# Delta stage: the gram products moved between the product through the state and the decay sums, and the block columns spread over six of eight chains

## The reference, cut to what matters

```python
# every token goes to 2 of 4 experts; each expert has a state S of 64x64 per head, 8 heads
def step(S, x):
    qt, kt, vt, bt, gt = x
    S = S * jnp.exp(gt)[..., None, None]
    kv = jnp.einsum('bhk,ebhkv->ebhv', kt, S)
    delta = (vt[None] - kv) * bt[..., None]
    S = S + kt[None, :, :, :, None] * delta[..., None, :]
    ot = jnp.einsum('bhk,ebhkv->ebhv', qt * scale, S)
    return (S, ot)
```

## Time and profile before

| | |
|---|---|
| runs | 3308.52, 3281.15, 3309.49 us; median 3308.52 |
| profiled execution | 3279.67 us, its span 3277.6 us, mean granted clock 0.964 |
| PE busy | 3008.8 us, 92% of the span |
| DVE busy | 1696.9 us, 52% |
| ACT, POOL busy | 1052.2 and 1480.7 us |
| the chain that ended last | 78% PE, 11% DVE, 4% issue, 3% ACT, 2% DMA |
| DVE L2114 and L2111 (block columns) | 114.5 and 98.7 us busy, 240 instructions each |
| the delta stage | from 1341 to 2012 us of the span |

### The profile page before, as it was taken

One profiled execution on the slowest core, in us unless ns is written; L12 is line 12 of the kernel. 1 busy time (PEld: TensorE's weight loads), 2 busy tenths in 40 slices (PEclk: granted clock), 3 DMA queues, 4 the chain that ended last, 5 costly groups with the idle time before them and its releaser, 6 DMA issues.

```text
span 3277.6 us, 45758 instructions
## 1 busy us (share of the span) xinstructions
PE 3008.8 (92%) x16145; PEld 1701.1 (52%) x16145; DVE 1696.9 (52%) x3820; ACT 1052.2 (32%) x2245; POOL 1480.7 (45%) x1466
## 2 busy tenths in 40 slices
PE   7999999888899899879999998998999999999828
PEld 3434566577677544457777765444533333444414
DVE  7633266488244432377766642442257777621361
ACT  2312422297122222233444432221034444432201
POOL 0565656498554447422222202554656666300003
PEclk9999999999999999999999989999999999999958
DMA  5400001110111244433444445311167666600404
GB/s 170 138 19 6 7 25 53 46 65 14 41 46 49 69 140 165 155 106 107 116 114 117 118 136 161 96 52 48 31 202 202 205 198 197 158 16 26 171 9 129
DMA packets 275957, 321.34 MB, mean 98 GB/s; under 512 B 155807, under 2 KB 193569, under 8 KB 275732
## 3 DMA queue, kind: packets, MB, share of 16 engines
q1 hardware_dynamic: 219684, 182.57, 18.5%
q0 software_dynamic: 51840, 134.60, 13.6%
q10 hardware_dynamic: 4208, 1.25, 0.2%
HBM read 215.75 MB, written 104.60 MB: 98 GB/s over the span
## 4 chain that ended last, share of the span: by engine, by line
PE 78%; DVE 11%; issue 4%; ACT 3%; DMA 2%; POOL 0%; SPq 0%; ACTq 0%; DVEq 0%; POOLq 0%
PE bank L2665 8%; PE bank L1520 5%; PE bank L2657 5%; PE bank L706 4%; PE bank L1299 3%; PE bank L2328 3%; PE bank L2819 3%; PE bank L2812 3%; PE bank L437 3%; PE bank L1115 3%; DVE delta_tmp L2111 2%; PE bank L729 2%; DVE delta_Us L2114 2%; PE bank L760 2%; PE bank L2308 2%
## 5 line engine op out<-in xcount | busy, mean ns | idle before, releaser
L2637 POOL DMA_INDIRECT conv_src<-xn_rows,keep x288 | 272.2, 945 | 175.3 <-DVE conv_msg L2703 109.4
L289 POOL DMA_INDIRECT sorted_bias<-perf_rec,place x256 | 259.2, 1012 | 146.5 <-PE bank L706 92.1
L2665 PE MATMUL bank<-conv_msg,conv_hot 128*128 128x512 f32 x576 | 272.0, 595 | 0.6 <-ACT conv_msg L2684 0.6
L1902 POOL TENSOR_TENSOR delta_dec<-delta_dec,rates_of 128x512 f32<-128x512 f32 x64 | 67.4, 1053 | 359.9 <-ACT delta_dec L1944 359.9
L2703 DVE TENSOR_TENSOR conv_msg<-bank,conv_src 128x512 f32<-128x512 f32 x288 | 185.5, 686 | 46.7 <-PE bank L2657 46.7
L664 POOL DMA_INDIRECT sorted_edge<-rec,place x128 | 126.7, 990 | 141.9 <-PE bank L1360 75.2
L2684 ACT ACTIVATE conv_msg<-conv_msg 128x1024 f32<-128x1024 f32 x144 | 152.0, 1055 | 102.0 <-DVE conv_msg L2703 102.0
L1115 PE MATMUL bank<-bias_prod,bias_hot 128*128 128x256 f32 x640 | 148.5, 388 | 25.2 <-issue 10.5
L2657 PE MATMUL bank<-conv_we,conv_eT 64*128 64x512 f32 x576 | 164.5, 648 | 0.7 <-ACT conv_eT L2681 0.7
L1099 POOL TENSOR_TENSOR bias_prod<-bias_col,bias_rec 128x512 f32<-128x512 f32 x128 | 146.9, 1177 | 17.1 <-PE bank L1115 16.4
L1115 PEld LDWEIGHTS bank<-bias_prod,bias_hot 128*128 128x128 f32 x640 | 120.4, 193 | 53.7 <-issue 28.6
(11 more groups left out here) (494 smaller groups left out, 6557.0 us busy)
## 6 DMA issues: line engine op xcount, KB each, us to landing
keep<-slot_qkv SPq DMA_DIRECT2D x32, 512.0 KB, 3.8
delta_kv<-slot_qkv SPq DMA_DIRECT2D x32, 512.0 KB, 3.8
sorted_edge<-sort_pad SPq DMA_DIRECT2D x8, 1440.0 KB
keep<-sorted_edge SPq DMA_DIRECT2D x18, 640.0 KB, 4.9
slot_out<-delta_o SPq DMA_DIRECT2D x64, 128.0 KB, 1.7
conv_src<-xn_rows,keep POOLq DMA_INDIRECT x288, 3.6
X<-in_x SPq DMA_DIRECT2D x4, 1024.0 KB, 10.9
sorted_bias<-perf_rec,place POOLq DMA_INDIRECT x256
```

The costliest lines, as they stand in the source:

```text
L289: POOL.indirect_dma_start(out=sorted_bias, out_offset=bass.IndirectOffsetOnAxis(ap=place[:, 0, c:c + 1], axis=0), in_=rec0[:, c, :], in_of ...
L2637: POOL.indirect_dma_start(out=src[:, n % 4, j, :], out_offset=None, in_=xn_rows, in_offset=bass.IndirectOffsetOnAxis(ap=rec[:, g % 3, k + ...
L2665: a = PE.matmul(bank[n % 2][:, :], hot[:, g % 2, k + j, :], msg[:, q, j, :], start=j == 0, stop=j == 1)
```

## The change

The gram products, at the end of a step before (0.85), are now issued between Z and the decay sums (0.21), and they, not the decay sums, wait for the transposed keys (`kq_ready`). BA moves from behind the step (1.0) into it (0.72). The inverse and the main part start one step later (MID and MAIN plus 1), so that the ahead part is 17 chains ahead. The block columns, spread over 4.6 steps before, are spread over six, at positions that leave the first 0.4 of each step free. "B out", "B in", "UL in", "L copy" and "blocks out" move with them.

```diff
-            MID, MAIN = 15.2, 16.2
+            MID, MAIN = 16.2, 17.2
...
-                for what, at in (("mask", -0.7), ("turn", -0.2), ("kq", -0.1), ("decay", 0.25), ("exp", 0.35), ("weigh", 0.45),
-                                 ("gram", 0.85), ("BA", 1.0),
-                                 ("Z", MID), ("Z copy", MID + 0.1), ("U", MID + 0.25), ("U copy", MID + 0.35),
+                for what, at in (("mask", -0.7), ("turn", -0.2), ("kq", -0.1), ("gram", 0.21), ("decay", 0.25), ("exp", 0.35),
+                                 ("weigh", 0.45), ("BA", 0.72),
+                                 ("Z", MID + 0.005), ("Z copy", MID + 0.1), ("U", MID + 0.25), ("U copy", MID + 0.35),
...
-                plan.append((2 * t + 2.2, "B out", t))
-                plan.append((max(2 * t + 13.4, 2 * BT * (t // BT) + 14.3), "UL in", t))
+                plan.append((2 * t + 1.8, "B out", t))
+                plan.append((max(2 * t + 14.4, 2 * BT * (t // BT) + 15.3), "UL in", t))
...
             for q in range(NBT):
                 first = 2 * BT * (q + 1)
-                plan.append((first + 0.6, "B in", q))
-                plan.append((first + 1.1, "blocks set", q))
+                plan.append((first + 0.4, "B in", q))
+                plan.append((first + 0.9, "blocks set", q))
                 for k in range(30, 0, -1):
-                    plan.append((first + 1.1 + 4.6 * (31 - k) / 31, "block column", (q, k)))
-                plan.append((first + 5.8, "L copy", q))
-                plan.append((first + 5.9, "blocks out", q))
+
+                    at = 0.6 + 6.0 * (31 - k) / 31
+                    plan.append((first + int(at) + 0.4 + 0.78 * (at - int(at)), "block column", (q, k)))
+                plan.append((first + 7.15, "L copy", q))
+                plan.append((first + 7.2, "blocks out", q))
...
                     if what == "decay":
                         PE.wait_ge(*masked.at(n + 1))
-                        PE.wait_ge(*kq_ready.at(n + 1))
...
                     if what == "gram":
+                        PE.wait_ge(*kq_ready.at(n + 1))
```

## The result

Four runs of the changed kernel took 3369.6 to 3382.5 us, median 3374.5, against 3309.0 for the kernel before (3281.2 to 3316.9): ratio 1.0238, interval 1.0193 to 1.0284. It is slower by 1.9 to 2.8%. The profiled execution took 3369.64 us, 90 more than the one before.

A forecast was written before the change was run, and what follows sets the result against it. The prediction took PE, busy 92% of the span, to bound the kernel. Its terms, 24 + 16 - 22 + 28 + 2 = +48 us on the median 3308.5, gave 3356.5 us, range 3300 to 3388.

The forecast's parts named there:

- both costs: Waits and low clock before the first inverse, 24 + 16 us; blocks' load behind a wait on SP, 28 us.
- the gain's two reasons: Heavy steps: 47 us of DVE work fit into 51.7, and the new order helps r; together 22 us.
- gain in the heavy steps: Six batches with block columns: PE no longer waits for DVE's late r, 22 us won.
- start, latency: Chains before the first inverse: nothing overlaps, 6.25 us a chain against 3.41; first L copy 24.2 us later.
- start, clock: Same first loop: idle gaps bring PE to 1.2 GHz in six of 14 chains, 16 us.
- late load, five batches: Third to seventh batch: "B in" waits behind "UL in"; stall 3.4 plus low clock 2.2 us each, 28 us.
- L copy to Z: L copy has slightly too little time before Z: 0.3 us a batch, 2 us for six.
- step moved to the tail: One step of 8.92 us gives way to a shorter tail step, offset by a late L copy: 0 us.
- (c): Low clock in the whole loop before the first inverse, 37 us there: +69 us, 3377; chance 0.15.
- (a): The waits are there but the clock holds at 2.4 GHz throughout: +21 us, 3330; chance 0.28.
- (b): "blocks set" finds the load in place, no five stalls, clock held: +4 us, 3312; chance 0.08.
- (d): DVE cannot place its columns, each heavy batch keeps its 3.7 us: +70 us, 3378; chance 0.07.

The follow-up runs named there:

- e9: The kernel before run again against itself, nothing changed: median 3305.5 us, ratio 1.0049.
- e1: The changed kernel with "B in" at 0.38 instead of 0.4, so issued ahead of "UL in": 3363.2 us, ratio 1.0098 to the kernel before.
- e6: The kernel before with only the new places of gram and BA, columns still over 4.6 steps: 3350.5 us, ratio 1.0054.
- e5: The kernel before with only the wider column spread (5.7 steps) and inverse and main parts one step later: 3332.8 us, ratio 0.9968.
- e4: The changed kernel with four unread matmuls behind each turn of chains 1 to 15: 3390.1 us, executed once.

## Why the prediction was right, step by step

The sign, the range (3300 to 3388) and the causes of both costs held; of the gain's two reasons one was needed. The sum, +48 us, was too small: the ratio says +79, and the trace 84 to 89 up to the last BA and 6 in the tail. Four of its terms were too small, and the base hid part of that. "I put the sum on the median, 3308.5": e9 shows what "two 28 us above it, which nothing in the profile explains" most likely were, executions with the long tail. The changed kernel's tail is of the short kind, so the sum belonged on 3279.67. There it gives 3328, against the 3369.64 of the changed kernel's profiled execution, 42 short, where 3356.5 was 18 short of the median. That the forecast came so close is luck in part: a base that lay 28 us too high met terms that were too low. The same mixture in the kernel before makes the ratio smaller than the traces do.

| term | forecast | measured |
|---|---|---|
| gain in the heavy steps | -22 | -18 to -23 (excess 20.4 to 25.1, and 2.2 in e1) |
| start, latency | +24 | about +26 |
| start, clock | +16 | about +26 |
| late load, five batches | +28 | +52 (changed kernel against e1, from BA of chain 17) |
| low clock behind the first Z | 0 | +3 |
| L copy to Z | +2 | +0.2 at the first; 2.2 in four steps of e1, counted in the first row |
| step moved to the tail | 0 | +5.7, or +4.0 with BA's shift put back |

**Gain.** Right in size, but the step that carried the argument was not needed. I had argued from the spread (47 us of work into 51.7) and named the order as a help. In e6 the order does it all, without the spread; in e5 the spread takes about 12 of the 20 us off the heavy steps and loses 15 at Z. I had priced the columns as before; their fall by POOL's rest was not in the forecast.

**Start.** The turn was forecast at 6.25 us and is 6.34. "I take six of 14" for the clock was the mis-sized part: twelve of the 14 turns, from the third on, were longer, by 2.2 us on average and not 2.66 (8.53 against 6.34), which makes 26. Rival (c), the low clock in the whole loop, was close: 37 forecast. Its reason holds too. I had argued that "after each fall PE's next long stretch of work brought the clock back"; it came back, but it fell again. The Trainium skill ("TensorE: Matmul & The Clock Gate", on the HAM clock gate) says that a loop which idles in every turn can start every turn cold. The trace here agrees, at 2.5 to 2.9 us of idle and 8.53 us a turn. The split is shown by e4 but for the fill's own 0.5 us a turn.

**Late load.** Place, cause and batches were as forecast. The stall was put at 3.4 and was 4.6 to 6.3 us. In the step shown above the DMAs of "UL in" took 4.5 us (3.4 forecast), and from "blocks set" to solve went 5.8 (4.6 forecast), since "blocks set" and a column, each beside POOL, took 2.01 and 1.03 in place of 1.22 and 0.21. The low clock behind the stall was put at 2.2 us; 52 us less the five waits' 25.5 and some 3 for the first of the waits for `Lf` leave under 5 each. The timeline of TensorE behind another of the stalls shows why:

```profile
1731.00:1738.00 7.00, 7.00 (x43) 6.32 (x44) 4.58 (x14) 1.36 (x3) 0.00 (x0) 0.50 0.16 33
1738.00:1745.00 7.00, 7.00 (x47) 4.82 (x46) 2.59 (x10) 0.91 (x3) 0.00 (x0) 0.50 0.27 85
1745.00:1752.00 7.00, 7.00 (x86) 5.01 (x84) 3.54 (x10) 3.02 (x8) 2.61 (x3) 0.88 0.16 26
```

For 14 us the granted clock is 0.50. I had taken it to return within the step.

**The tail.** "One step of 8.92 gives way to one of the tail's" was forecast at nothing, and the tail is 5.7 us longer, 1.7 of it BA's shift. In stretches of 10 us from the last BA the clock is 0.82, 0.50, 0.50 and 0.82 (13.6 us lost), before it was 0.71, 0.50 and 0.94 (8.5): that is 5.1 for the clock, and the step itself comes out about 1 us shorter than 8.92, as forecast. The kernel before varies by 28 in the same place.

**Rivals.** (a), a clock that holds, is out by 0.74 in the start. (b), a load in time, is e1; it was not the changed kernel. (d), columns that do not fit, is out: mid-batch steps are 8.92. The 70 us of (d) would have come as near to the result as (c); the steps, and not the time, decide between them.

## What to carry to other kernels

When a step is moved ahead of another in an in-order schedule, write down the loop for the part of the run where nothing else is in flight; an order that is free in the full pipeline can be the whole chain at its start. When two steps fall on the same position, look at what the one in front waits for, and at who stands behind the one that then waits. A short fix for either is a different order for the first turns, and a few hundredths of a step. Price an idle gap of PE with its clock: here it doubled what the waits alone cost. When half of a change is tried alone, look for what that half breaks before its sum is read. And read what a kernel does against itself before a difference of half a per cent is believed.

## What the runs showed of the hardware that was not expected

Gaps of 2.5 to 2.9 us in turns of 6.3 us brought PE's clock down to 1.2 GHz for part of each turn from the third on, and four matmuls of 0.9 us in each gap kept it at 2.4 GHz and brought the first L copy 17 us forward. A stall of 4.95 us was followed by 14 us at 1.2 GHz, though PE was busy all the time, and in the tail of the kernel before the clock stayed there for some 17 us in one execution and some 85 in another, in which PE was busy for 58.7 of 60 us. The same 480 column instructions took 213 us on DVE before, and 168 in the changed kernel: 121 and 41 of them ran beside a POOL instruction, the others took the same 0.33 to 0.34 us in both.
